# Four of the eight blocks of probabilities per pair turned by a plain product with the identity

## The chip, the cores and the metric

One Trainium2 chip, one of its cores. The metric is the device time of one execution in microseconds (us). The kernel before took 412.27 us, the median of three runs (411.49 to 414.54).

The engines are named as in the profile: PE is TensorE's product, PEld its load of the stationary operand, DVE VectorE, ACT ScalarE, POOL GpSimd, and SP the engine whose queue issues most transfers.

## The reference

The computation is one block of a vision transformer on 64 images of 96 x 96 pixels with three channels, all inputs and outputs in fp32.

```python
# patches: 16 x 16 x 3 = 768 values, 36 per image, plus one class row: T = 37 tokens per image
x = layernorm(patches) ; x = x @ W + bias ; x = layernorm(x) + posemb      # D = 256
h = concat(class_row, x)                                                   # [64, 37, 256]
q, k, v = split(layernorm(h) @ Wqkv + bqkv)    # 16 heads of 16, rotary embedding on q and k
probs = softmax(q @ k.T / 4)                   # per image and head: 37 x 37
h = h + (probs @ v) @ Wout + bout
# feed-forward: 256 -> 1024 -> 256, ternary weights, activations rounded to 8 bits
h = h + bitlinear(gelu(bitlinear(layernorm(h), W1, b1)), W2, b2)
```

The change touches one thing only: how `probs` is turned, before `probs @ v`, so that its source tokens lie on the partitions.

## The kernel before, in words

The 64 x 37 = 2368 token rows are worked on in three stages that follow each other on every engine.

**Patch stage** (up to some 168 us). 18 tiles of 128 rows and one of 64: normalise, turn the pixels on TensorE (L369), multiply by W (L379), normalise again, form queries, keys and values (L416, L396), rotate, and turn queries and keys (L424). The values go to DRAM (`vsc`) and are loaded again pair by pair. While this stage ends, the first attention steps are mixed into it: the scores of pair 0, a last patch step, the scores of pair 1, another last patch step.

**Attention stage** (some 168 to 313 us). The 64 images are taken as 32 pairs (`NP`). The two images of a pair lie on partitions 0 to 36 and 64 to 100 (`SPAN` = 101 rows); the probabilities of a pair are one buffer `pr` of 101 rows and 16 heads x 64 columns. The order is written out by hand and the same on each engine: step s does one part for each of four pairs.
- TensorE (L500 to L510): the scores of pair s (L464, 16 small products of 32 x 37 by 74 columns); the two turns of the attended rows of pair s-3 (`turn_out`, L484), bank 5 ahead of bank 4; the product of probabilities and values of pair s-2 (`attend`, L496, 16 products of 101 x 37 by 34 columns); the eight turned blocks of the probabilities of pair s-1 (`turn_probs`, L468 to L476), four into PSUM bank 4 and then four into bank 5. Each block is 101 rows by 101 columns of `pr` and holds two heads. The last of each four raises a semaphore, `p_turned4` or `p_turned5`.
- VectorE (L783): reciprocal and scaling of pair s-3 (L775, L779), then maximum (L764) and subtraction (L768) of pair s.
- ScalarE (L1007): the two evacuations of the turned attended rows of pair s-3 (L993), which also wait for `p_turned4` and `p_turned5` of pair s-1 since they share those banks; the two evacuations of the turned probabilities of pair s-1 (`probs_out`, L1000); the exponential of pair s (L1005).
- SyncE loads the values of pair p into one of four buffers once pair p-4 has been attended (L312).

`turn_out` waits for both evacuations of the probabilities of pair s-2 (`p_evac4`, `p_evac5`, L481), because it writes into the same two banks. `attend` waits for them too (L488, L489). The scores of pair s wait for the subtraction of pair s-1 (L456).

**Feed-forward stage** (from some 313 us). 19 tiles again: output product (L531), turn (L539), up product in bf16 (L548), turn (L557), down product in bf16 (L565), with rounding on ScalarE and VectorE. Its first output product is issued while the last attention steps drain.

Every turn of the kernel is `pe.transpose(out, in, ident)`: the data are the stationary operand and the 128 x 128 identity `ident`, or its top left part, is the moving one.

Of the kernel before, what the change touches and what calls it, by code (L numbers as in the profile page):

```python
# [33 lines left out]
SPAN = 64 + TOK  # L34
# [63 lines left out]
def vit_block(nc, a, out):  # L98
    with ExitStack() as ctx:
# [8 lines left out]
        ident = tab[:, 0:128]  # L108
# [70 lines left out]
        ps = ctx.enter_context(nc.psum_tensor("ps", [128, 8, 512], F32))  # L179
# [49 lines left out]
        def war(eng, s, t, behind=2):  # L229

            if not isinstance(t, int) or t >= behind:
                eng.wait_ge(S[s], t - behind + 1)
# [109 lines left out]
        def _(pe):  # L342
# [3 lines left out]
            for k in range(KP):  # L346
                mm = pe.matmul(ps[0:K3, 6, 0:D], bass.AP(byp, k, [[2 * KP + 2, 128], [0, K3]]), w_raw[:, k, :],
                               start=(k == 0), stop=(k == KP - 1))
# [119 lines left out]
            def turn_probs(p, b):  # L468
                pe.wait_ge(S["s_exp"], p + 1)
                war(pe, f"p_evac{b}", p, 1)  # L470
                for g in range(4):
                    at0 = 2 * 64 * (4 * (b - 4) + g)
                    flat = pr[p % 2][0:SPAN, :, :].rearrange("p h t -> p (h t)")
                    mm = pe.transpose(ps[0:SPAN, b, SPAN * g:SPAN * g + SPAN], flat[:, at0:at0 + SPAN],  # L474
                                      ident[0:SPAN, 0:SPAN])
                mm.then_inc(S[f"p_turned{b}"], 1)  # L476

            def turn_out(p, b):
# [21 lines left out]
            def attention_step(s):  # L500
                if live(s, NP):
                    scores(s)
                if live(s - 3, NP):
                    turn_out(s - 3, 5)
                    turn_out(s - 3, 4)
                if live(s - 2, NP):
                    attend(s - 2)
                if live(s - 1, NP):
                    turn_probs(s - 1, 4)
                    turn_probs(s - 1, 5)  # L510
# [724 lines left out]
```

## Time and profile before

| what | value |
|---|---|
| median of three runs | 412.27 us (411.49 to 414.54) |
| the profiled execution | 409.72 us |
| its span, first to last instruction | 407.9 us |
| mean granted TensorE clock | 0.816 of full speed |
| busy: PE, PEld | 352.7 us (86%), 268.9 us (66%) |
| busy: DVE, ACT, POOL | 248.6 us (61%), 218.5 us (54%), 134.1 us (33%) |

The profile is of one execution, 2.55 us below the median of the runs; 1.8 us of its time lie outside its span. A step of a stage is read from that one execution, and a difference found in it is then set against the median. Matmuls are pipelined, and the record of one covers its latency too, so a group of n records is shorter than n times the mean of one. The granted clock is given per stretch, as a share of full speed: 1.00 is 2.4 GHz and 0.50 is 1.2 GHz.

### The profile page before, as it was taken

What the parts mean: (1) busy time and instruction counts of PE and PEld (TensorE: products, weight loads), DVE (VectorE), ACT (ScalarE), POOL (GpSimd) and SP (SyncE); (2) the same over time, 40 slices, a digit from 0 to 9 for tenths busy, and PEclk for the clock granted to TensorE, in tenths of its full rate; (3) what the DMA queues carried; (4) which work ended last, traced back from release to release, by engine and by line L of the source; (5) the groups of instructions that cost most, each with busy time, mean ns of one, the idle gap of its engine ahead of it and who ended that gap; (6) DMA issues with size and microseconds to landing.
All of it is one profiled execution on the core that took longest, in us unless ns stands there. A gap on an engine that the chain in (4) does not pass through costs nothing.

```text
span 407.9 us, 9528 instructions
## 1 busy us (share of the span) xinstructions
PE 352.7 (86%) x3564; PEld 268.9 (66%) x3564; DVE 248.6 (61%) x641; ACT 218.5 (54%) x423; POOL 134.1 (33%) x247
## 2 busy tenths in 40 slices
PE   0748889999999999789999998998988689999984
PEld 0536777787776555467777777777776467777653
DVE  1385775676665533545545545545542799999984
ACT  2443545775554444343344344344333499999994
POOL 4233543454453454291000000000000646566550
PEclk9978999999999999955555555555555999999999
DMA  8993320000000011210011110110000000101011
GB/s 240 355 400 110 134 73 7 22 15 27 15 27 15 29 41 41 65 24 22 23 34 24 24 32 22 24 33 22 24 12 2 0 2 14 40 27 40 26 41 58
DMA packets 18892, 22.31 MB, mean 55 GB/s; under 512 B 2272, under 2 KB 15600, under 8 KB 18848
## 3 DMA queue, kind: packets, MB, share of 16 engines
q1 hardware_dynamic: 17792, 19.53, 14.9%
q10 hardware_dynamic: 1056, 2.18, 1.8%
q8 instruction: 29, 0.48, 0.5%
q14 instruction: 15, 0.12, 0.1%
HBM read 16.68 MB, written 5.02 MB: 53 GB/s over the span
## 4 chain that ended last, share of the span: by engine, by line
PE 59%; DVE 15%; ACT 11%; issue 6%; POOL 4%; DMA 2%; ACTq 0%; DVEq 0%; POOLq 0%
PE ps L379 12%; PE ps L474 12%; PE ps L496 9%; PE ps L416 8%; ACT ximg L1000 5%; DVE sc L825 4%; PE ps L484 4%; DVE ximg L844 3%; PE ps L369 3%; PE ps L396 3%; DMA qkT<-in_W 2%; PE ps L362 2%; ACT xT L910 2%; ACT ximg L1047 1%; DVE qa L707 1%
## 5 line engine op out<-in xcount | busy, mean ns | idle before, releaser
L1080 POOL TENSOR_TENSOR rs<-rs,nhalf 128x1 f32<-128x1 f32 (+1 forms) x76 | 41.9, 559 | 235.4 <-DVE rs L819 157.8
L993 ACT ACTIVATE qkT<-ps 128x74 f32<-128x74 f32 x64 | 14.7, 233 | 85.5 <-PE ps L474 81.3
L379 PE MATMUL ps<-w_in,xT 128*128 128x256 f32 (+1 forms) x228 | 55.0, 392 | 4.9 <-ACT xT L910 4.9
L764 DVE TENSOR_REDUCE ximg<-ps 101x16 f32<-101x592 f32 x32 | 24.7, 773 | 51.8 <-PE ps L464 51.8
L474 PE MATMUL ps<-tab,ximg 101*101 101x101 f32 x256 | 53.1, 386 | 0.2 <-ACT ximg L1005 0.2
L379 PEld LDWEIGHTS ps<-w_in,xT 128*128 128x128 f32 (+1 forms) x228 | 42.4, 193 | 13.5 <-ACT xT L910 7.4
L474 PEld LDWEIGHTS ps<-tab,ximg 101*101 101x101 f32 x256 | 45.3, 282 | 2.4 <-ACT ximg L1005 0.3
L496 PEld LDWEIGHTS ps<-ximg 101*37 101x37 f32 x1024 | 35.0, 174 | 7.0 <-issue 7.0
L496 PE MATMUL ps<-ximg 101*37 101x34 f32 x1024 | 39.4, 255 | 0.0
L416 PE MATMUL ps<-w_qk,hnT 128*128 128x512 f32 (+1 forms) x76 | 36.4, 601 | 1.6 <-DVE qb L715 1.6
L707 DVE TENSOR_TENSOR qa<-ps,tab 128x512 f32<-128x512 f32 (+1 forms) x19 | 13.1, 689 | 39.5 <-PE ps L362 39.5
L910 ACT ACTIVATE xT<-ps 128x768 f32<-128x768 f32 (+1 forms) x19 | 15.1, 795 | 38.5 <-PE ps L369 38.5
L1087 POOL TENSOR_TENSOR qa<-qa,qb 128x512 f32<-128x512 f32 (+1 forms) x19 | 24.1, 1268 | 17.0 <-DVE qb L715 17.0
L484 PE MATMUL ps<-tab,ximg 101*128 101x101 f32 x64 | 18.2, 387 | 12.4 <-ACT ximg L1000 12.4
L464 PE MATMUL ps<-qkT 32*37 32x74 f32 x1024 | 23.5, 321 | 2.6 <-DVE ximg L768 1.3
L768 DVE TENSOR_TENSOR ximg<-ps,ximg 101x592 f32<-101x592 f32 x32 | 24.8, 776 | 1.1
L1047 ACT ACTIVATE ximg<-ximg,magic,sc 128x1024 f32<-128x1024 f32 (+1 forms) x19 | 23.6, 1241 | 2.3 <-DVE sc L837 1.8
L844 DVE SCALAR_TENSOR_TENSOR ximg<-ps,sc,wide 128x1024 f32<-128x1024 f32 (+1 forms) x19 | 24.4, 1282 | 0.6 <-PE ps L548 0.6
L548 PE MATMUL ps<-w1t,ximg 128*128 128x512 bf16 (+1 forms) x76 | 19.7, 382 | 5.5 <-ACT ximg L1036 5.4
L1000 ACT ACTIVATE ximg<-ps 101x296 f32<-101x296 f32 x64 | 23.1, 417 | 2.4 <-PE ps L474 2.4
L825 DVE TENSOR_REDUCE sc<-ximg 128x1 f32<-128x1024 f32 (+1 forms) x19 | 22.9, 1207 | 2.1 <-ACT ximg L1042 1.6
L557 PE MATMUL ps<-tab,ximg 128*128 128x128 f32 (+1 forms) x152 | 19.7, 272 | 5.2 <-ACT ximg L1047 5.2
(105 smaller groups left out, 678.7 us busy)
## 6 DMA issues: line engine op xcount, KB each, us to landing
ximg<-in_x SPq DMA_DIRECT2D x18, 384.0 KB, 12.8
ximg<-vsc SPq DMA_DIRECT2D x64, 51.0 KB, 1.9
vsc<-vt SPq DMA_DIRECT2D x18, 136.0 KB, 1.7
out<-ximg SPq DMA_DIRECT2D x18, 128.0 KB, 1.7
ximg<-in_W SPq DMA_DIRECT2D x2, 1024.0 KB, 6.3
wide<-in_rows ACTq DMA_DIRECT2D x1, 768.0 KB, 13.4
w_qk<-in_Wqk SPq DMA_DIRECT2D x1, 512.0 KB, 13.4
qkT<-in_offsets ACTq DMA_DIRECT2D x1, 448.0 KB, 11.4
```

The source lines that it names most:

```text
L379: pe.matmul(dst[0:n, :], xT[t % 2][:, k, 0:n], w_in[:, k, :], start=(k == 0), stop=False)
L416: pe.matmul(ps_qk[0:n, :], hnT[t % HB][:, k, 0:n], w_qk[:, k, :], start=(k == 0), stop=False)
L474: mm = pe.transpose(ps[0:SPAN, b, SPAN * g:SPAN * g + SPAN], flat[:, at0:at0 + SPAN], ident[0:SPAN, 0:SPAN])
L484: pe.transpose(ps[:, b, O_AT:O_AT + SPAN], at[p % 4][0:SPAN, 128 * m:128 * m + 128], ident[0:SPAN, 0:SPAN]).then_inc(S[f"o_turned{b}"], 1)
L496: mm = pe.matmul(dst.rearrange("p (e c) -> p e c", e=2), pT[p % 2][0:SPAN, g, i, :], rhs, start=True, stop=True)
L764: v.tensor_reduce(mx[u][0:SPAN, :].rearrange("p (r h) -> p r h", r=4), ps_s, AX.X, ALU.max).then_inc(S["s_max"], 1)
L768: v.tensor_tensor(pr[u][0:SPAN, :, 0:TOK].rearrange("p (r h) t -> p r h t", r=4), ps_s, mx[u][0:SPAN, :].rearrange("p (r h) -> p r h", r=4 ...
L825: v.tensor_reduce(sc[t % 8][0:n, c:c + 1], src[0:n, :], AX.X, ALU.max, apply_absolute_value=True).then_inc(S[f"{x}_amax"], 1)
L844: v.scalar_tensor_tensor(out=hd[t % 3][0:n, :], in0=ps_f[0:n, :], scalar=sc[t % 8][0:n, 3:4], in1=fb1[0:n, :], op0=ALU.mult, op1=ALU.add). ...
L1000: act.activation(pT[p % 2][0:SPAN, g0:g0 + 4, :, :], ps_pT(b), ACT.Copy).then_inc(S[f"p_evac{b}"], 1)
L1047: act.activation(hd[t % 3][0:n, :], hd[t % 3][0:n, :], ACT.Identity, bias=magic[0:n, :], scale=sc[t % 8][0:n, 6:7]).then_inc(S["f_rnd"], 1)
L1080: pool.tensor_tensor(rs[u][0:n, i:i + 1], rs[u][0:n, i:i + 1], nhalf[0:n, :], ALU.pow).then_inc(S[done], 1)
```

## The change

`turn_probs` turns the four blocks of bank 4 as before. The four blocks of bank 5 become plain products: the same stationary operand (101 x 101 of the probabilities), the same moving operand (the identity, 101 x 101), the same place in PSUM, but without the transpose mode. Order, waits, semaphores and every other instruction stay as they are.

```diff
@@ def turn_probs(p, b):
                 for g in range(4):
                     at0 = 2 * 64 * (4 * (b - 4) + g)
                     flat = pr[p % 2][0:SPAN, :, :].rearrange("p h t -> p (h t)")
-                    mm = pe.transpose(ps[0:SPAN, b, SPAN * g:SPAN * g + SPAN], flat[:, at0:at0 + SPAN],
-                                      ident[0:SPAN, 0:SPAN])
+                    dst, part = ps[0:SPAN, b, SPAN * g:SPAN * g + SPAN], flat[:, at0:at0 + SPAN]
+                    if b == 4:
+                        mm = pe.transpose(dst, part, ident[0:SPAN, 0:SPAN])
+                    else:
+                        mm = pe.matmul(dst, part, ident[0:SPAN, 0:SPAN], start=True, stop=True)
                 mm.then_inc(S[f"p_turned{b}"], 1)
```

## Rows read from the trace of the kernel before

**Rows 1.** The page: busy time and share, and PE's busy tenths and granted clock in 40 slices.
```profile
PE 352.7 (86%) x3564; PEld 268.9 (66%) x3564; DVE 248.6 (61%) x641; ACT 218.5 (54%) x423; POOL 134.1 (33%) x247
...
PE   0748889999999999789999998998988689999984
...
PEclk9978999999999999955555555555555999999999
```

**Rows 2.** The chain of waits over one attention step: start us, us, what.
```profile
224.87 1.63 PE ps L474 x8
226.50 0.02 issue
...
226.71 0.73 ACT ximg L1000 x2
...
227.52 0.57 PE ps L484 x2
228.09 1.16 PE ps L496 x32
229.25 1.63 PE ps L474 x8
```

**Rows 3.** The timeline of attention steps: start us, us, engine, line, operation, operands, count.
```profile
180.91 1.68 PE L474 MATMUL ps<-tab,ximg 101*101 101x101 f32 x8
...
226.41 0.75 PE L464 MATMUL ps<-qkT 32*37 32x74 f32 x32
...
308.14 1.68 PE L474 MATMUL ps<-tab,ximg 101*101 101x101 f32 x8
```

**Rows 4.** Stretches: length, busy PE, PEld, DVE, ACT, POOL (instructions), PEclk, DMA share, GB/s.
```profile
169.40:173.00 3.60, 1.45 (x40) 1.14 (x40) 3.40 (x7) 1.81 (x4) 1.22 (x1) 1.00 0.44 111
173.00:176.40 3.40, 2.01 (x56) 1.62 (x58) 1.30 (x3) 2.01 (x6) 3.31 (x3) 0.50 0.00 0
312.70:316.30 3.60, 3.33 (x11) 2.40 (x10) 1.86 (x6) 0.93 (x3) 0.00 (x0) 0.50 0.01 2
224.87:229.25 4.38, 4.02 (x75) 3.31 (x75) 2.23 (x4) 1.68 (x5) 0.00 (x0) 0.50 0.12 28
...
316.34:319.75 3.41, 2.19 (x11) 1.34 (x10) 2.21 (x9) 0.67 (x1) 2.34 (x6) 1.00 0.00 0
```

**Rows 5.** A feed-forward stretch, PE alone: all lines, then L557, then L539.
```profile
340.00:360.00 20.00, 19.06 (x132) 1.00 0.10 35
...
340.00:360.00 20.00, 5.18 (x40) 1.00 0.10 35
...
340.00:360.00 20.00, 1.91 (x10) 1.00 0.10 35
```

**Rows 6.** The timeline of the first attention steps.
```profile
168.26 0.49 PE L464 MATMUL ps<-qkT 32*37 32x74 f32 x32
...
169.74 0.78 DVE L768 TENSOR_TENSOR ximg<-ps,ximg 101x592 f32<-101x592 f32 x1
...
170.66 0.49 PE L464 MATMUL ps<-qkT 32*37 32x74 f32 x32 [1.33 <-DVE ximg L768]
...
171.32 0.96 PE L474 MATMUL ps<-tab,ximg 101*101 101x101 f32 x8 [0.17 <-ACT ximg L1005]
```

**Rows 7.** The timeline of the output products, at half and at full clock.
```profile
312.69 2.07 PE L531 MATMUL ps<-w_o,qkT 128*128 128x256 f32 x4
...
317.77 1.10 PE L531 MATMUL ps<-w_o,qkT 128*128 128x256 f32 x4 [0.61 <-DVE h L803]
```

**Rows 8.** The chain of waits in the patch stage: W's products of one tile.
```profile
90.54 2.59 PE ps L379 x12
```

**Rows 9.** The timeline of PEld in two neighbouring stretches of 0.16 us.
```profile
225.26 0.46 PEld L474 LDWEIGHTS ps<-tab,ximg 101*101 101x101 f32 x2
...
225.43 0.46 PEld L474 LDWEIGHTS ps<-tab,ximg 101*101 101x101 f32 x2
```

## The prediction

> **What bounds the kernel now.** I read the page first: PE is busy for 86% of the span, and its granted clock is at 5 tenths in 15 slices of 40, the whole attention stage, and near full elsewhere [rows 1]. The reader is to see that a third of the run goes at 1.2 GHz.
>
> Next the chain of waits over one attention step [rows 2]. It is a loop without slack. The eight turned blocks of a pair take 1.63 us; ScalarE follows, and until the next PE work on the chain 1.02 us pass (226.50 to 227.52), most of it the two evacuations (0.73 us); then the two turns of attended rows, 0.57 us; then attend, 1.16 us; then the next pair's blocks. Sum: 4.38 us. The scores (226.41, 0.75 us) lie inside ScalarE's stretch [rows 3] and are free. DVE is busy 2.23 us of the step and ACT 1.68 us [rows 4]: neither is near the bound. From the blocks at 180.91 to those at 308.14 [rows 3] there are 127.23 / 4.387 = 29 equal steps; with the one ahead of them and the one behind, 31.
>
> Then the clock, stretch by stretch [rows 4]. It fell at 173 us, after 3.6 us in which PE had been busy 1.45. Afterwards PE was busy 4.02 of 4.38 us in every step, and the clock stayed at 0.50 to the end of the stage. It came back at 316.3, after 3.6 us with PE busy 3.33, so with the same busy share as in the attention steps. What differs is the kind of work: there mostly plain products of 128 x 128 by 256 columns [rows 7]; in the attention steps transposes (L474, L484) and plain products that use a small part of the array, 32 x 37 and 101 x 37 [rows 2, 3]. In the feed-forward stage transposes are 7.09 of 19.06 us of PE's busy time beside plain full-array products, and the clock is 1.00 [rows 5]. So PE's busy time as such does not hold the clock; large plain products do, by these rows.
>
> **The change part by part.** *The products themselves.* A plain fp32 product is issued as two records, each with a weight load: the output product of a tile is two products (k = 0, 1) and shows four records [rows 7]. At full clock a record of 256 columns takes 2.59 / 12 = 0.216 us [rows 8], 0.84 ns per column, with its weight load hidden under the record ahead; 101 columns are 0.085 us, a product 0.17. A transposed block is one record, and at half clock two of them start 0.17 us apart [rows 9], so about 0.085 at full clock. A plain turned block therefore costs twice a transposed one: 0.34 against 0.17 us at half clock, 0.17 against 0.085 at full. Four of them: **+0.68 us per step at half clock, +0.34 at full**. All of it is on the loop: ScalarE's evacuations of both banks stand behind L993 of bank 5, which waits for `p_turned5`. Bounds at half clock: +0.68 if all loads stay hidden (as in rows 7 and 8), and +2.0 us if each of the eight records also shows its own load (the loads of rows 9 are 0.17 apart, so one is no longer than that: 8 x 0.17 = 1.36 on top). Below 0.68 nothing: the columns have to be streamed. I take the hidden case, since both plain rows show it.
>
> *What is queued behind.* PE's scores of the next pair move later by the same amount, but stay inside ScalarE's stretch. VectorE's two passes follow the scores and feed a block a whole step later. No DMA is moved; the loads of values are four pairs ahead. No wait is added.
>
> *The clock.* The plain blocks are eight records of 101 rows by 101 columns per step, over three quarters of the array in rows and in columns. Kind and size lie much nearer to the products of rows 7 than to the 32 x 37 and 101 x 37 ones. I take it that they bring the clock back to 1.00 within the first steps. What one step then costs comes from rows at both levels:
> - the blocks: eight transposes took 0.96 us at full clock [rows 6] and 1.68 at half [rows 3], so the chain's 1.63 becomes 0.91; plus 0.34: 1.25;
> - ScalarE's stretch: unchanged, 1.02;
> - the two turns: 0.57 x 0.96 / 1.68 = 0.33;
> - attend: no row at full clock. The scores, also small products, went from 0.49 to 0.75 [rows 6, 3], a ratio of 0.65: 0.76. Bounds: 0.58 (halved) and 1.16 (not scaled);
> - sum 3.36 us, **1.02 less than now**. With the ends for turns and attend (halved; not scaled): 3.14 and 4.00.
>
> What is late next: the loop over scores, maximum and subtraction, 168.26 to 170.66 = 2.40 us [rows 6], and DVE's 2.23 us. Both lie below 3.36.
>
> *The sum.* I give three steps to half clock before it rises (the start-up gaps at 170 to 175 stay): 3 x 0.68 = +2.0. 28 steps at full clock: 28 x -1.02 = -28.6. The first output product finds the full clock, 1.10 instead of 2.07 [rows 7]: -1.0. Total -27.6 us: 409.7 becomes 382 in terms of the profiled execution, and 412.3 becomes **384.7** in terms of the median; I write 384, since the clock may not fall at all. Its own range: 31 x -1.24 - 1.0 = -39, so 373; 28 x -0.38 + 2.0 - 1.0 = -9.6, so 402.
>
> The Trainium skill ("TensorE: Matmul & The Clock Gate", Part 4) says that a transpose does not count as activity of TensorE in the way a matmul does, so that the clock does not go to full for it. By that rule the trace agrees: 0.50 through steps that are 92% busy [rows 4].
>
> **The rivals.** *A, the clock stays at 0.50: slower.* The place is the attention stage. The four plain blocks only cost: 31 x 0.68 = +21 us, **433 us** (with the upper bound, 31 x 2.0: 474). It decides if the activity that the chip sees in a step stays below what brought the clock back at 316 us. For it: the plain blocks fill 1.35 us of a step of 5.06 us, the rest is small products, transposes and waits, while at 312.7 to 316.3 the full-array products filled more than half. The small products of every step have never lifted the clock. Against it: with attend and scores around them, plain work of some kind would fill 1.35 + 1.16 + 0.75 us of 5.06, against 1.91 of 4.38 before. Chance 0.17.
>
> *C, the clock changes between both levels, or rises late.* For it: a step at full clock has gaps, and the clock fell once in gaps (169.4 to 173.0) [rows 4]. With half of the steps at each level: 15.5 x (0.68 - 1.02) = -5 us, **407 us**. Chance 0.05.
>
> *D, a plain fp32 block costs four transposed ones.* Rows 8 and 9 say two: 0.84 ns per column and record, two records, against 0.17 us for 101 columns at half clock. If it were four, a step at full clock would be 3.36 + 0.68 = 4.04 and one at half clock 2.04 longer than now: 28 x -0.34 + 3 x 2.04 - 1 = -4.4, **408 us**, and with the clock at half 31 x 2.04 = +63 us. Chance 0.03. This is the rule of the Trainium skill that speaks against the change ("TensorE: Matmul & The Clock Gate", Terms): transpose mode is four times faster for fp32.
>
> *That the change does not do what it says:* if a plain product with the identity came out as the same single record, nothing would change. Rows 7 exclude it, as every plain fp32 product there shows two.
>
> **How the numbers follow.** Forecast 0.75, A 0.17, C 0.05, D 0.03. 384 is the forecast's own number, with 373 to 402 as its own range. For 8 in 10 the range is 373 to 410: the forecast within its bounds (0.73), C and the better half of D (0.07). A is left out. A measurement of this kernel can tell about 1% from no change (408.1 to 416.4 us is "within"). Faster by over 1%: 0.75 + 0.03 of C + 0.01 of D = 0.79. Within 1%: 0.04. Slower: A, 0.17.
>
> **What the profile of the changed kernel would show.** Granted clock 1.00 in the attention stage: right, and 0.50 there: A. L474's counterpart for bank 5 with eight records per step, 0.085 us apart at full clock or 0.17 at half: the price is right; 0.34 and D holds. Steps 3.4 us apart; attend at 0.76. ScalarE's evacuations at 0.73 as before, and the scores inside ScalarE's stretch. The output product at 2.07 us at the start of the feed-forward stage would say that the clock was not back. The prediction is wrong if the clock stays at 0.50 although the plain blocks fill a quarter of the step, or if at full clock another loop than the one of rows 2 sets the step.

## The result, and the profile after

The changed kernel took 436.0 us, the median of four runs (435.48 to 437.12), against 411.9 us (410.12 to 414.54) for the kernel before in the same set: ratio 1.058, 95% interval 1.052 to 1.065. It is 24 us slower. I had forecast 384 us. Rival A, the clock stays at 0.50, had 433 us and a chance of 0.17. Ratios here and below compare only runs within 1.5% of the fastest of the same kernel, and none is given where half of a kernel's runs lie outside.

The page of the changed kernel, busy time and granted clock in 40 slices of 10.9 us:

```profile
PE 378.2 (87%) x3692; PEld 292.2 (67%) x3692; DVE 248.7 (57%) x641; ACT 218.4 (50%) x423; POOL 133.9 (31%) x247
...
PEclk9979999999999999555555555555555599999997
```

The clock is at 0.5 through the whole attention stage, as before [rows 1], in 16 slices instead of 14, and the slices are longer. PE has 128 records more: 32 pairs x 4 blocks, two records each instead of one.

The chain of waits over one attention step of the changed kernel (L476 the transposed blocks, L478 the plain ones, L1003 the evacuations, L487 the two turns, L499 attend):

```profile
233.47 0.93 PE ps L476 x4
234.40 1.37 PE ps L478 x8
...
235.98 0.73 ACT ximg L1003 x2
236.71 0.09 issue
236.80 0.57 PE ps L487 x2
237.37 1.16 PE ps L499 x32
238.53 0.93 PE ps L476 x4
```

From 233.47 to 238.53 are 5.06 us, against 4.38 [rows 2]. The blocks take 2.30 us instead of 1.63; evacuations, turns and attend are the same to 0.01 us. So the price of the plain blocks is what the prediction gave for half clock, 0.68 us, and nothing else in the chain of a step moved.

The end of the stage, in stretches of the changed kernel (length, busy PE, PEld, DVE, ACT, POOL, PEclk, DMA share, GB/s), and its output products in the timeline:

```profile
334.80:348.00 13.20, 11.15 (x33) 6.64 (x30) 6.26 (x23) 3.20 (x6) 4.59 (x11) 0.50 0.00 1
348.00:352.00 4.00, 2.36 (x13) 1.52 (x12) 3.34 (x7) 1.91 (x3) 1.99 (x5) 0.99 0.00 0
```
```profile
334.89 2.08 PE L534 MATMUL ps<-w_o,qkT 128*128 128x256 f32 x4
...
343.52 2.05 PE L534 MATMUL ps<-w_o,qkT 128*128 128x256 f32 x4 [0.61 <-DVE h L806]
...
348.28 1.03 PE L534 MATMUL ps<-w_o,qkT 128*128 128x256 f32 x4
```

The first output product starts at 334.89, and four of them run at half clock; the clock is back only at 348. In the kernel before it was back 3.6 us after the first one (312.69 to 316.3) [rows 4, 7]. Its timeline has the fifth output product, the one that starts at 348.28 above, here:

```profile
322.47 1.03 PE L531 MATMUL ps<-w_o,qkT 128*128 128x256 f32 x4
```

The spans differ by 434.4 - 407.9 = 26.5 us, and this is where they go. Attention, from the blocks of pair 1 (178.04 here, 176.93 before) to the first output product: 156.85 against 135.76 us, **21.1 us = 31 x 0.68**. The feed-forward stage from there on: 99.5 against 95.2 us, 4.3 us. Of these 3.6 are the late return of the clock: the fifth output product starts 13.39 us after the first one (348.28 - 334.89), and 9.78 us in the kernel before (322.47 - 312.69). The other 0.7 us were not traced. The remaining 1.1 us of the difference lie ahead of the first scores (169.37 against 168.26 [rows 6]), before the change has done anything.

### The profile page after: what moved, and what is told of

The parts are those of the page before. It is cut to its first block, busy times and chain, and to the rows that moved or that the text cites. A ratio compares the mean times of both kernels' runs of the same rounds, so it can differ in the third digit from the quotient of the medians.

```text
span 434.4 us, 9784 instructions
## 1 busy us (share of the span) xinstructions
PE 378.2 (87%) x3692; PEld 292.2 (67%) x3692; DVE 248.7 (57%) x641; ACT 218.4 (50%) x423; POOL 133.9 (31%) x247
## 4 chain that ended last, share of the span: by engine, by line
PE 62%; DVE 15%; ACT 13%; issue 5%; DMA 3%; POOL 1%; ACTq 0%; DVEq 0%
PE ps L379 12%; PE ps L478 10%; PE ps L499 9%; PE ps L416 8%; PE ps L476 7%; DVE sc L828 5%; ACT ximg L1003 5%; PE ps L487 4%; DVE ximg L847 3%; PE ps L369 3%; DMA qkT<-in_W 3%; ACT ximg L1050 3%; PE ps L396 2%; PE ps L534 2%; PE ps L362 2%
## 5 line engine op out<-in xcount | busy, mean ns | idle before, releaser
L478 PE MATMUL ps<-tab,ximg 101*101 101x101 f32 x256 | 49.5, 372 | 0.0
L478 PEld LDWEIGHTS ps<-tab,ximg 101*101 101x101 f32 x256 | 46.8, 288 | 0.0
L499 PEld LDWEIGHTS ps<-ximg 101*37 101x37 f32 x1024 | 35.0, 174 | 7.0 <-issue 7.0
L499 PE MATMUL ps<-ximg 101*37 101x34 f32 x1024 | 39.4, 255 | 0.0
L476 PE MATMUL ps<-tab,ximg 101*101 101x101 f32 x128 | 31.7, 401 | 0.2 <-ACT ximg L1008 0.2
L487 PE MATMUL ps<-tab,ximg 101*128 101x101 f32 x64 | 18.2, 387 | 12.4 <-ACT ximg L1003 12.4
L476 PEld LDWEIGHTS ps<-tab,ximg 101*101 101x101 f32 x128 | 23.8, 276 | 2.4 <-ACT ximg L1008 0.3
L534 PE MATMUL ps<-w_o,qkT 128*128 128x256 f32 (+1 forms) x76 | 23.7, 441 | 1.5 <-DVE h L806 1.5
```

The lines of the kernel that those rows point to most:

```text
L476: mm = pe.transpose(dst, part, ident[0:SPAN, 0:SPAN])
L478: mm = pe.matmul(dst, part, ident[0:SPAN, 0:SPAN], start=True, stop=True)
L487: pe.transpose(ps[:, b, O_AT:O_AT + SPAN], at[p % 4][0:SPAN, 128 * m:128 * m + 128], ident[0:SPAN, 0:SPAN]).then_inc(S[f"o_turned{b}"], 1)
L499: mm = pe.matmul(dst.rearrange("p (e c) -> p e c", e=2), pT[p % 2][0:SPAN, g, i, :], rhs, start=True, stop=True)
L534: pe.matmul(ps_z[0:n, :], qkT[:, k, 128 * t:128 * t + n], w_o[:, k, :], start=(k == 0), stop=False)
```

## The experiments

**What is asked.** Theory 1: more work is needed to bring the clock back than to hold it; it falls in the start-up gaps of the attention stage, and four plain blocks cannot bring it back. Theory 2: the plain blocks nearly did it, and a little more plain work would. All times are medians, ratios against the kernel before in the same set.

**1. All eight blocks plain** (`all8`; the edit is set against the changed kernel).

```diff
-                    if b == 4:
-                        mm = pe.transpose(dst, part, ident[0:SPAN, 0:SPAN])
-                    else:
-                        mm = pe.matmul(dst, part, ident[0:SPAN, 0:SPAN], start=True, stop=True)
+                    mm = pe.matmul(dst, part, ident[0:SPAN, 0:SPAN], start=True, stop=True)
```

> All eight blocks of a pair are turned by the plain product (the changed kernel turns four so). Theory 1, the plain blocks are paid in full and are far from enough to bring the clock back: granted clock stays at 0.50, each step gets 0.68 us longer again (5.07 to 5.75 us), total 436 + 31 x 0.68 = 457 us. Theory 2, the four plain blocks only just missed: with eight the clock returns to 1.00, a step takes 0.24 + 8 x 0.17 + 1.02 + 0.33 + 0.76 = 3.7 us, total about 392 us.

Measured: four runs of 388.4, 393.0, 406.8 and 406.9 us (median 399.9), with mean granted clocks of 0.987, 0.974, 0.926 and 0.928. All four lie below the fastest run of the kernel before in the same set, 409.7 us. The page of the 393.0 us run, and its chain at half clock, then at full clock (L475 the blocks):

```profile
PEclk9988999999999999995799999999999999999999
```
```profile
186.52 2.99 PE ps L475 x16
```
```profile
201.85 0.40 PE ps L484 x2
...
202.98 1.61 PE ps L475 x16
...
205.64 0.40 PE ps L484 x2
```

The clock fell, and came back after some steps; after that a step took 205.64 - 201.85 = 3.79 us. Theory 2's number, 392, is the nearer one. With eight plain blocks the clock does return, and the kernel is faster than the one before although each block costs double. Only one of the four runs has a trace; that the clock returned at different moments is read from the mean clocks alone. So the mechanism that I had predicted exists; four blocks are on the wrong side of it.

**2. Six of eight plain** (`a_six`).

```diff
-                    if b == 4:
+                    if b == 4 and g < 2:
```

> Six of the eight blocks of a pair plain (two of bank 4, four of bank 5). With four the clock stayed at 0.50, with eight it came back. If it is a matter of the amount of plain work per step: either still 0.50, with 5.41 us per step and 436 + 31 x 0.34 = 446 us, or 1.00 after some steps with 3.57 us per step and 388 to 400 us. Theory 1 (the amount is what decides, and it is nearly reached at eight): the run to run spread is large, with late returns, mean between 400 and 446.

Measured 442.4 us (440.9 to 447.7), ratio 1.078, interval 1.069 to 1.086; clock 0.5 through the stage. Six blocks do not bring the clock back either, and cost more. They cost 6.4 us more than four, where 31 x 0.34 = 10.5 were expected, because the second output product was already at full clock here (1.10 us, at 347.13), which takes back some 4 us of the late return above. The large spread that Theory 1's wording asked for did not show.

**3. Keep the clock from falling** (`b_start`): the kernel before, with plain products whose results nobody reads, only where PE had been idle in the start-up.

```diff
+            def warm(n, bank, at0):
+                for _ in range(n):
+                    pe.matmul(ps[:, bank, at0:at0 + 240], pos_rows[:, 0:128], hot[:, 0:240], start=True, stop=True)
...
             pe.wait_ge(S["v_evac"], NT + 1)
+            warm(10, 4, 0)
             attention_step(1)
+            pe.wait_ge(S["a_init"], 1)
+            warm(6, 6, 272)
             patch_step(NT + LAG + 2)
+            warm(10, 6, 272)
             pe.wait_ge(S["a_init"], 2)
```

> The kernel before, all blocks transposed, with 26 additional plain bf16 products (111 x 128 by 240 columns, results unused) placed only in PE's start-up gaps of the attention stage (between 169 and 175 us): 10, 6 and 10. They cost about nothing in time. If what matters is that the clock fell in those gaps and less work is needed to hold the clock than to bring it back, the clock stays at 1.00 through the stage and a step takes about 3.0 us: 412 - 31 x 1.36 = 370 us. If the work of the steps itself does not hold the clock, it falls to 0.50 a few us after the gaps and the time is 409 to 414 us.

Measured 369.3 us, two runs 0.07 us apart, ratio 0.896 (0.888 to 0.905). Its page and the chain of one step (L474 the eight transposed blocks, L1008 the evacuations, L484 the turns, L496 attend):

```profile
PEclk9996999999999999999999999999969999999999
```
```profile
228.51 0.90 PE ps L474 x8
...
229.63 0.72 ACT ximg L1008 x2
...
230.44 0.41 PE ps L484 x2
230.85 0.72 PE ps L496 x32
231.57 0.90 PE ps L474 x8
```

This is the experiment that settles most. The 26 products lie before 175.2 us. After them the stage runs 94 us with the same eight transposes and the same small products per step as before [rows 2, 3], and the clock stays at 1.00; a step takes 3.06 instead of 4.38 us. The stretch, as in rows 4:

```profile
175.20:269.40 94.20, 75.30 (x2260) 63.11 (x2260) 67.46 (x123) 51.07 (x151) 9.74 (x6) 1.00 0.15 35
```

The same steps that never brought the clock back in 140 us, with PE busy for 92% of them, hold it once it is up, with PE busy for 80%.

**4. Only the first two gaps filled** (`b_gap12`: 10, 6 and 0 products).

> The kernel before with additional products in the first two start-up gaps only (10 and 6, up to 173.5 us), and the third gap (174 to 175) left empty. If the first two gaps alone make the clock fall: 1.00 through the stage, 369 us. If each gap does: the clock falls a few us later than in the kernel before and stays at 0.50, 408 to 412 us.

Measured 410.6 us (408.8 to 412.6), ratio 0.998 (0.995 to 1.001). The page: the clock falls one slice later and stays down.

```profile
PEclk9978999999999999965555555555555999999999
```

So the third gap by itself is enough to make it fall, and the first two together are enough too, since in the kernel before the clock fell ahead of the third; once down it is not brought back. 16 products bought nothing, the 10 more of `b_start` bought 41 us.

**5. The changed kernel with the start-up gaps filled** (`a_start`: the edit of 3 on the changed kernel).

> The changed kernel (four of eight blocks plain) with 26 additional plain products (10, 6 and 10; 111 x 128 by 240 columns, bf16, results unused) in the start-up gaps only. Theory 1 (the clock is held by less work than brings it back; the change failed only because the clock had fallen before it): the clock stays at 1.00, a step takes 3.06 + 0.34 = 3.40 us, total 369.3 + 31 x 0.34 = 380 us. Rival (the plain blocks help to hold the clock, or cost less beside a full clock): below 372 us. If the clock falls all the same: 436 us.

Measured 381.3 us (379.9 to 383.9), ratio 0.928 (0.923 to 0.933). One step (L476 transposed, L478 plain, L1011 evacuations, L487 turns, L499 attend):

```profile
228.25 0.73 ACT ximg L1011 x2
...
229.06 0.40 PE ps L487 x2
229.47 0.72 PE ps L499 x32
230.19 0.53 PE ps L476 x4
230.72 0.73 PE ps L478 x8
...
231.66 0.73 ACT ximg L1011 x2
```

A step is 231.66 - 228.25 = 3.41 us, against 3.06 with eight transposes. At a clock that is up, the four plain blocks cost 0.35 us per step and bring nothing.

**6. The same with six products more in each step** (`b_start_step`, `a_start_step`).

```diff
             def attention_step(s):
                 if live(s, NP):
                     scores(s)
+                if live(s - 2, NP):
+                    war(pe, "o_norm", s - 2)
+                    warm(6, 6 + s % 2, 272)
```

> The kernel before, with the 26 additional products in the start-up gaps and in each step six more (111 x 128 by 240 columns, bf16, results unused) between the scores and the turn of the attended rows, where PE waits for ScalarE. If full-array plain work holds the clock: 1.00 through the stage, a step of 3.0 to 3.2 us, 370 to 378 us. If it does not: 0.50, the six products take 1.2 us at half clock of which 0.3 lie in the wait, so 31 x 0.9 = 28 us more, 440 us.

> The changed kernel (four of eight blocks plain) with the same additional products in the start-up gaps and in each step. It gives the price of the four plain blocks at full clock if the clock stays up: +0.34 us per step over the same kernel with eight transposes, 31 x 0.34 = +10.5 us. If the plain blocks cost four times a transposed one: +1.0 us per step, +31 us. If the clock is at 0.50: +0.68 us per step, +21 us.

Measured 368.6 us (ratio 0.894, 0.886 to 0.903) and 378.9 us (0.920, 0.911 to 0.928): +10.3 us for the plain blocks, where 31 x 0.34 = 10.5 were expected. Six large products per step cost nothing beside the same kernel without them (369.3): they lie in the wait for ScalarE, and a step still takes 3.06 us.

**7. The six products, without filling the gaps** (`b_step`). The edit is that of 6 on the kernel before.

> The kernel before with six additional products in each step, in the wait for ScalarE, and none in the start-up gaps, so that the clock falls at 173 us as before. Theory 1 (bringing it back wants nearly continuous full-array work): the clock stays at 0.50, the six cost 1.2 us per step of which 0.3 lie in the wait, 412 + 28 = 440 us. Rival (six large products per step bring it back): the clock is at 1.00 after a few steps, about 372 us.

Measured 373.9 us (372.7 and 375.1), ratio 0.909 (0.904 to 0.914). Here the rival holds and Theory 1's strong form falls: the clock went down at 173 as in the kernel before and was back within two steps. The blocks of two neighbouring steps in the timeline, at half and at full clock:

```profile
178.45 1.68 PE L474 MATMUL ps<-tab,ximg 101*101 101x101 f32 x8
...
183.51 0.96 PE L474 MATMUL ps<-tab,ximg 101*101 101x101 f32 x8
```

The six products in the chain of the first of these steps:

```profile
180.82 1.31 PE ps L502 x6
```

They took 1.31 us of PE at half clock, the four plain blocks of the changed kernel 1.37. Nearly the same time, the opposite outcome. The next runs ask what differs.

**8. Type, size, amount and place of the six products.** Each changes one thing of `b_step`, except that the fp32 products also use all 128 rows of the array instead of 111, and that `b_step_small` cuts rows and columns together.

```diff
 b_step_f32:   3 x  w_qk[:, 0, 0:128] by w_qk[:, 0, 0:120]   (fp32, six records)
 b_step_id:    3 x  w_qk[:, 0, 0:128] by ident[:, 0:120]     (the same, identity as moving operand)
 b_step_small: 6 x  pos_rows[0:101, 0:101] by hot[0:101, 0:240]
 b_step3:      3 x  pos_rows[:, 0:128] by hot[:, 0:240]
 b_pos:        6 x  as in b_step, behind turn_probs(s - 1, 5) instead of behind the scores
```

> As the kernel with eight transposes and six additional bf16 products per step (373.9 us), but with three fp32 products of 128 x 128 by 120 columns in their place, which stream for the same time (six records of 240 clocks of the array). If the type of the operand does not matter: the clock returns, about 374 us. If fp32 work counts for less than bf16 work of the same duration, and this is why the four plain blocks failed: 0.50, about 440 us.

> The kernel with three additional fp32 products of 128 x 128 by 120 columns per step (377.2 us), with columns of the identity as the moving operand instead of weights; size, type, count and place are the same. If the values matter: the clock stays at 0.50, about 435 us. If they do not: the clock comes back, 372 to 380 us.

> The same with the six additional bf16 products cut to 101 x 101 of the array (from 111 x 128), the size of the plain blocks, same place and duration. If the part of the array in use decides: 0.50 and about 440 us. If not: the clock returns, about 374 us.

> Three additional products of 111 x 128 per step instead of six, behind the scores. If half the amount is too little: 0.50; 0.3 of their 0.6 us lie in the wait, 412 + 31 x 0.3 = 421 us. If it is enough: about 372 us.

> Eight transposes and six additional bf16 products of 111 x 128 per step, now right behind the turned blocks (the place of the plain blocks) instead of behind the scores. If the place does not matter: the clock comes back, about 374 us. If it does: 0.50 and about 435 us.

| kernel | what is changed of b_step | us (range) | ratio, 95% interval | clock in the attention stage |
|---|---|---|---|---|
| b_step | - | 373.9 (372.7 to 375.1) | 0.909 (0.904 to 0.914) | back within two steps |
| b_step_f32 | fp32 | 377.2 (375.1 to 379.3) | 0.915 (0.907 to 0.924) | back after four steps |
| b_step_id | fp32, moving values are the identity | 372.1 (368.4 to 375.9) | - | back |
| b_pos | place | 377.2 (372.6 to 381.7) | - | back |
| b_step_small | 101 x 101 of the array instead of 111 x 128 | 435.0 (434.3 to 435.6) | 1.056 (1.048 to 1.063) | 0.50 to the end |
| b_step3 | three instead of six | 413.7 (413.6 to 413.8) | 1.006 (1.004 to 1.009) | 0.50 to the end |

The pages of `b_step`, then of `b_step_small`:

```profile
PEclk9997999999999999998699999999999999999998
```
```profile
PEclk9968999999999999555555555555555899999997
```

Neither fp32, nor the identity as moving operand, nor the other place kept the clock down; `b_step_id` and `b_pos` are two runs each, all four below 382 us. The amount matters, and so does the part of the array: the same six products, at the same place, bring the clock back with 111 x 128 in use and fail with 101 x 101, the size of the plain blocks, although they take a little longer there. Whether rows or columns decide was not separated. Nor is it PE's idle time that makes the two failures: in `b_step_small` (its six products in the chain, then a stretch as in rows 4) and in `b_step3` (the last row) PE is never idle, at 0.50.

```profile
227.30 1.37 PE ps L502 x6
```
```profile
180.00:300.00 120.00, 120.00 (x1876) 104.16 (x1876) 51.71 (x93) 39.17 (x117) 5.12 (x3) 0.50 0.10 23
```
```profile
224.00:233.00 9.00, 9.00 (x156) 7.41 (x154) 4.47 (x8) 3.36 (x10) 0.00 (x0) 0.50 0.12 27
```

**9. The plain blocks over more of the array.** `a_wide` takes 128 columns of the stationary operand, `a_full` 128 rows too; `a_dense` and `a_full_dense` put a dense weight block in place of the identity in the changed kernel and in `a_full`, and so leave out the turn of these blocks. That changes the moving operand; the stationary one stays the probabilities.

```diff
 a_wide:  pe.matmul(ps[:, b, SPAN * g:SPAN * g + SPAN], flat[:, at0:at0 + 128], ident[0:SPAN, 0:SPAN], ...)
 a_full:  pe.matmul(ps[:, b, SPAN * g:SPAN * g + SPAN], whole[:, at0:at0 + 128], ident[:, 0:SPAN], ...)
```

> The changed kernel with its four plain blocks widened from 101 to 128 columns of the stationary operand (the 27 additional result rows are unused); the moving columns, and so PE's time, are the same. If the number of array columns in use counts: the clock returns, 381 to 395 us. If not, or not enough: 436 us as the changed kernel.

> The changed kernel with its four plain blocks over the whole array: 128 rows (27 more rows of the probabilities' buffer, multiplied by zeros of the identity) and 128 columns of the stationary operand, moving columns unchanged. PE's time as in the kernel widened to 128 columns (1.72 us for eight records at half clock, 5.42 us per step). If the part of the array in use decides: the clock comes back as with the six 111 x 128 products, then 3.5 us per step and 385 to 400 us. If the place in the step or something else decides: 0.50 and 442 us.

> The changed kernel with a dense weight block in place of the identity as the moving operand of the four plain blocks of 101 x 101 (the turn of these blocks is left out so). If the identity's zeros are why they fail: the clock comes back, 381 to 400 us. If the size or the amount is: 0.50, 436 us.

> The same with the four plain blocks over the whole array of 128 x 128 (the turn of these blocks is left out). If the identity's zeros are why a_full failed: the clock comes back, 385 to 400 us. If the amount is still too small: 0.50, 442 us.

Measured: 442.0 us (1.073, 1.068 to 1.077), 442.9 us (1.077, 1.075 to 1.079), 435.9 and 443.0 us. All at 0.50 through the stage. Using the whole array alone does not make four blocks enough, nor do the identity's zeros explain it. The chain of `a_wide`, its eight plain records:

```profile
226.91 1.72 PE ps L478 x8
```

They take 0.215 us each instead of 0.17, for the same 101 moving columns, where the expectation had PE's time unchanged; this makes the attention stage of `a_wide` and `a_full` 31 x 0.35 = 11 us longer than that of the changed kernel. The total of `a_wide` is only 6 us longer: its second output product was already at full clock.

```profile
345.20 2.08 PE L535 MATMUL ps<-w_o,qkT 128*128 128x256 f32 x4
...
348.10 1.10 PE L535 MATMUL ps<-w_o,qkT 128*128 128x256 f32 x4 [0.38 <-DVE h L807]
```

**10. The drain** (`b_start_drain`): `b_start` with eight products in each of the last two steps, where the page of `b_start` shows a short dip.

```diff
+                if NP <= s < NP + 2:
+                    war(pe, "o_norm", s - 2)
+                    warm(8, 6 + s % 2, 272)
```

> The kernel before with the 26 products in the start-up gaps and eight more in each of the two last steps, where the stage drains (the clock fell to 0.50 for 6.8 us there in the kernel with the start-up gaps filled). If that fall is due to the gaps of the drain, the clock stays at 1.00, attend and the first output product are again 0.72 and 1.10 us instead of 1.16 and 2.00, and some 2 us go: 367 us. If not: 369.

Measured 367.8 us (367.2 to 369.6), ratio 0.895 (0.892 to 0.898). The first output product, in `b_start` and then here:

```profile
272.39 2.00 PE ps L539 x4
```
```profile
270.72 1.06 PE ps L542 x4
```

So the dip at the end was due to the gaps of the drain: with them filled the clock is at 1.00 from 269 to 273 us, in `b_start` at 0.50 from 269.5 to 276. This version has the lowest median, 43 us below the kernel before, with every block turned by a transpose. The times alone do not set it apart from `b_start_step` (368.6) and `b_start` (369.3): its own runs reach up to 369.6.

## Why the prediction was wrong

**The step that failed** is the one of the clock: "Kind and size lie much nearer to the products of rows 7 than to the 32 x 37 and 101 x 37 ones. I take it that they bring the clock back to 1.00 within the first steps." They did not in any of the 31 steps. I had read the rows on the clock as a question of kind, and settled it by likeness. The runs show a question of amount and of the part of the array together, which the likeness could not answer: eight plain blocks bring the clock back, six and four do not; six products of 111 x 128 do, three do not, six of 101 x 101 do not. The rows of before held the warning: the products that brought the clock back filled most of 3.6 us [rows 4, 7], while four plain blocks fill 1.37 of 5.06. I had written that under rival A, and gave it 0.17.

**What was missed beside it.** I asked only what would bring the clock back, and took the start-up gaps as given. The prediction concludes from rows 5 that large plain products hold the clock. `b_start` shows otherwise: the steps of the kernel before, which have none, hold it at 1.00 for 94 us. The fall at 173 us was in my rows, with its place and with what PE did before it (busy 1.45 of 3.60 us [rows 4]), and I used it only for two microseconds of start-up cost.

**Terms that were right.** The price of a plain block, twice a transposed one: 0.68 us per step at half clock (5.06 - 4.38), 0.35 at full (3.41 - 3.06), against 0.68 and 0.34. Rival D, four times, falls. The Trainium skill ("TensorE: Matmul & The Clock Gate", Terms) has transpose mode four times faster for fp32; for these blocks the runs show twice, and the measurement decides. The step at full clock with four plain blocks: 3.36 forecast, 3.41 in `a_start`; attend 0.76 forecast and 0.72 measured, the two turns 0.33 and 0.40. `a_start` took 381.3 us where the forecast, under the condition that the clock is up, gave 384. So nearly the whole error is the condition. Rival A's 433 is right in its mechanism, 31 x 0.68 = 21 us, and missed that the clock also came back later in the feed-forward stage, 3.6 us in the profiled execution.

**Two slips in the working.** The page of rows 1 has the clock at 5 tenths in 14 slices, where the prediction counts 15, and the upper end of the forecast's own range, 9.6 us off 412.3, comes to 403 and not 402. Neither changes the forecast.

**The rule on transposes.** The Trainium skill ("TensorE: Matmul & The Clock Gate", Part 4) says that transposes do not count towards the clock as matmuls do. No run here contradicts it for bringing the clock back: 92% busy steps at 0.50 [rows 4]. But steps with eight transposes hold 1.00 for 94 us (`b_start`), with small plain products beside them; which of the two holds it was not separated.

**What stays open.** Why four blocks over the whole array (`a_full`, eight records, 1.72 us of a 5.4 us step) fail where three fp32 products of 128 x 128 (`b_step_f32`, six records, 1.56 us) succeed. One difference left is that PE has no wait at all in a step of `b_step_f32` at half clock, and in `a_full` 0.4 us for ScalarE, with records that follow each other more slowly than their columns stream. The wait alone cannot be it: `all8` has one of 0.4 us in each step of 5.74 us at half clock and succeeds, `b_step3` and `b_step_small` have none and fail. Another difference was never varied: the stationary operand. In `a_full` it holds probabilities, with zeros in 54 of its 128 columns (the zeroed columns 37 to 63 of each head, L1126), in `b_step_f32` weights. The moving values were tested, these were not. Nor was it tried why the clock came back 13 us after the first output product in the changed kernel and in `a_dense`, and within 4 us in the kernel before, in `a_six`, `a_wide` and `a_full`. And some kernels that bring the clock back from 0.50 have runs far apart: 18 us in `all8`, 9 us in `b_pos`, 7 us in `b_step_id`. One trace of each is on record, so the cause of that spread is not shown.

## What to carry to other kernels

When a stage runs at half clock, look first at where the clock fell, not at the work of the stage: a few idle microseconds at its start may be the cause, and filling them with unused products costs nothing (26 of them, 41 us here). Work that holds a clock need not be able to bring it back, so test the two apart. Do not pay for the clock on the critical path: the plain blocks cost 0.35 us per step even where it is up, while products in a wait for another engine are free as long as they fit into it. At full clock the six did; at half clock they outgrew it (`b_step_small`: 5.16 us per step instead of 4.38).

## What the runs showed of the hardware

- A stage of the same instructions has two stable speeds: 4.38 us per step at 0.50 and 3.06 us at 1.00, depending on a few microseconds ahead of it (`b_gap12` and `b_start` differ in 10 products before 175 us, and by 41 us).
- The same time on PE does not count the same: six 240-column products of 111 x 128 per step bring the clock back (`b_step`, 373.9 us), six of 101 x 101 do not (`b_step_small`, 435.0 us).
- Plain fp32 records with 128 stationary and 101 moving columns follow each other at 1.72 / 8 = 0.215 us at half clock, those with 101 and 101 at 0.17 us. 0.215 us is 258 clocks of 1.2 GHz, two for each stationary column, so the weight load seems to set the pace there, which is an estimate from these two times. Transposes with 128 stationary and 101 moving columns do not show that pace: the two turns of attended rows follow each other at 0.17 us (L484, 0.34 us for both in the chain of `b_step_small`).
